# Fetching some tiles row by row from SyncE and ScalarE in two edge sums of a graph network

## The reference

```
def _rel_graph_conv(h, basis, coeff, bias, src, dst, etype, norm):
    W = jnp.einsum('rb,bdf->rdf', coeff, basis)
    Hr = jnp.einsum('nd,rdf->nrf', h, W)
    msg = Hr[src, etype] * norm
    agg = jax.ops.segment_sum(msg, dst, num_segments=N)
    return agg + bias
h = jax.nn.relu(_rel_graph_conv(feat, ...1, src, dst, etype, norm))
out = _rel_graph_conv(h, ...2, src, dst, etype, norm)
...
h = jnp.matmul(x, weight)
weighted = h[src] * edge_weight[:, None]
aggregated = jax.ops.segment_sum(weighted, tgt, num_segments=num_nodes)
in_deg = jax.ops.segment_sum(edge_weight, tgt, num_segments=num_nodes)
```

## Time and profile before

| | us |
|---|---|
| median of 3 runs | 9475.49 |
| lowest and highest | 9473.54, 9476.48 |
| the profiled execution | 9459.24 |
| its span | 9457.5 |

### The profile page before, as it was taken

The page is one execution under the profiler, slowest core; times in us unless marked ns, Lnnn a source line. Parts: engine busy times, 40 slices in busy tenths (PEclk is TensorE's granted clock), DMA queues, the critical chain, the costliest instruction groups (busy, mean ns, idle before and its releaser), DMA issues. The chain is left out here.

```text
span 9457.5 us, 158810 instructions
## 1 busy us (share of the span) xinstructions
PE 7101.5 (75%) x35186; PEld 5063.2 (54%) x35186; DVE 5926.1 (63%) x21108; ACT 3121.1 (33%) x10505; POOL 6656.1 (70%) x7024
## 2 busy tenths in 40 slices
PE   6555546666686666669999957777677777799999
PEld 4222224343343333334444446666566666799999
DVE  7666645444434444446665567777677777799888
ACT  2222210000020000000000045555455555699998
POOL 3777777777725777767777767777577777477776
PEclk9999999999995555555555567777777777899999
DMA  4222223111153111111111122222122222211111
GB/s 111 89 88 87 85 78 99 53 53 53 53 217 105 53 53 53 53 54 52 53 53 53 50 60 60 60 60 60 51 60 60 60 60 60 84 53 53 52 52 51
DMA packets 292477, 636.18 MB, mean 67 GB/s; under 512 B 124830, under 2 KB 160801, under 8 KB 279585
## 3 DMA queue, kind: packets, MB, share of 16 engines
q0 software_dynamic: 223872, 420.21, 16.8%
q1 hardware_dynamic: 68032, 210.12, 6.5%
HBM read 478.99 MB, written 150.87 MB: 67 GB/s over the span
## 5 line engine op out<-in xcount | busy, mean ns | idle before, releaser
L1058 POOL DMA_INDIRECT relsum_rows<-relation_table,tab_idx x1994 | 1891.0, 948 | 836.8 <-issue 496.1
L1101 PE MATMUL relsum_sums<-relsum_hot,relsum_rows 128*128 128x128 f32 x3988 | 1556.5, 498 | 930.8 <-DMA relsum_rows<-relation_table,tab_idx 689.0
L1101 PEld LDWEIGHTS relsum_sums<-relsum_hot,relsum_rows 128*128 128x128 f32 x3988 | 994.4, 312 | 1490.0 <-DMA relsum_rows<-relation_table,tab_idx 1477.6
L1001 POOL DMA_INDIRECT conv_rows<-tensor_table,src_idx x997 | 943.6, 946 | 404.2 <-issue 213.6
L1058 POOL DMA_INDIRECT gcnsum_rows<-x_table,src_idx x997 | 952.5, 955 | 333.5 <-issue 178.2
L1001 POOL DMA_INDIRECT gat2sum_rows<-gat_table,src_idx x997 | 944.4, 947 | 303.8 <-issue 235.5
L1001 POOL DMA_INDIRECT gat1sum_rows<-gat_table,src_idx x997 | 943.7, 947 | 303.8 <-issue 222.7
L668 POOL DMA_INDIRECT records<-sort_recs,place_rows x968 | 927.1, 958 | 295.1 <-issue 295.1
L1068 DVE TENSOR_SCALAR relsum_hot<-iota_row,dst_rel,w 128x128 f32<-128x128 f32 x1994 | 708.9, 356 | 429.1 <-issue 419.7
L1101 PE MATMUL gcnsum_sums<-gcnsum_hot,gcnsum_rows 128*128 128x128 f32 x1994 | 781.6, 495 | 0.0
L2095 ACT ACTIVATE conv_rows_attr<-conv_rows,conv_rec 128x64 f32<-128x64 f32 x2991 | 754.9, 334 | 50.5 <-SPq L2054 43.7
(11 more groups left out here) (392 smaller groups left out, 15104.0 us busy)
## 6 DMA issues: line engine op xcount, KB each, us to landing
relation_table<-table_row SPq DMA_DIRECT2D x30, 2048.0 KB, 6.3
relation_table<-sort_space SPq DMA_DIRECT2D x40, 1024.0 KB
relsum_rows<-relation_table,tab_idx POOLq DMA_INDIRECT x1994, 2.5
place_lo_wide<-lo_rows SPq DMA_DIRECT2D x121, 256.0 KB, 3.4
relation_table<-place_extra SPq DMA_DIRECT2D x20, 1024.0 KB
gcnsum_rows<-x_table,src_idx POOLq DMA_INDIRECT x997, 2.5
gat1sum_rows<-gat_table,src_idx POOLq DMA_INDIRECT x997, 2.5
gat2sum_rows<-gat_table,src_idx POOLq DMA_INDIRECT x997, 2.5
```

Of the source, the lines that this page charges most:

```text
L1001: pool.indirect_dma_start(bufs[:, t % depth, :], None, table, bass.IndirectOffsetOnAxis(ap=idx[:, t:t + 1], axis=0)).then_inc(landed[t % l ...
L1058: pool.indirect_dma_start(rows[:, t % depth, :], None, table, bass.IndirectOffsetOnAxis(ap=idx[:, t:t + 1], axis=0)).then_inc(landed[t % d ...
L1101: pe.matmul(bank[:, 0:P], rows[:, t % depth, :], hot[:, t % HOTS, :], start=True, stop=True).then_inc(s["multiplied"], 1)
```

## The change

A new class, `RowByRow`, fetches every 80th tile of a sum from another engine. It first writes the row numbers of its tiles, a few columns of the index tile, to device memory, and reads them back into one partition. For each of its tiles it then loads 16 numbers at a time into registers (8 loads) and issues 128 DMAs, each for one row of 512 bytes. It has two buffers; the fetch of its third tile and each later one waits until its tile two before is multiplied.

In the second relational sum SP fetches 12 tiles (79, 159, ... 959) and ACT 10 (119, 199, ... 839); in the graph sum SP fetches 12 (79, ... 959). POOL leaves these tiles out, its other tiles keep their buffers, and PE waits for these tiles on the semaphores of the fetching engine. The first relational sum is as it was.

```diff
+class RowByRow:
+    STEP = 80
...
+    def landed_at(self, t):
+        n = self.tiles.index(t)
+        return self.landed[n % 2], 16 * P * (n // 2 + 1)
...
+    def program(self, eng, multiplied, multiplied_at):
+        last = self.tiles[-1]
+        eng.dma_start(self.listed.rearrange("n p -> p n"), self.idx[:, self.first:last + 1:self.STEP],
+                      allow_slow_non_contiguous=True).then_inc(self.list_out, 16)
+        eng.wait_ge(self.list_out, 16)
+        eng.dma_start(self.numbers[:, :], self.listed.rearrange("(o n) p -> o (n p)", o=1)).then_inc(self.list_in, 16)
+        eng.wait_ge(self.list_in, 16)
+
+        def fetch(n, j):
+            for c in range(0, P, 16):
+                numbers = self.env.nc.values_load_multi_w_load_instructions(
+                    self.numbers[0:1, bass.ds(n * P + c, 16)], engines=[ENGINES[self.kind]], min_val=0,
+                    max_val=self.table.shape[0] - 1, skip_runtime_bounds_check_because="the records hold row numbers of the table")[1]
+                for e in range(16):
+                    eng.dma_start(self.rows[c + e:c + e + 1, j, :], self.table[bass.ds(numbers[e], 1), :]).then_inc(self.landed[j], 16)
+
+        for j in range(2):
+            fetch(j, j)
+        with eng.Fori(1, self.count // 2) as i:
+            for j in range(2):
+                eng.wait_ge(multiplied, i * (2 * self.STEP) + multiplied_at(self.first + (j - 2) * self.STEP + 1))
+                fetch(i * 2 + j, j)
...
             beside.sync(sp)
+            if "SP" in by_row:
+                by_row["SP"].program(sp, s["multiplied"], v["multiplied"])
...
                 beside.pool_at(pool, t)
+                if t in side_of:
+                    continue
...
             beside.act(act)
+            if "ACT" in by_row:
+                by_row["ACT"].program(act, s["multiplied"], v["multiplied"])
...
-                pe.wait_ge(landed[t % depth].sem, landed[t % depth].at(16 * (t // depth + 1)))
+                if t in side_of:
+                    pe.wait_ge(*side_of[t].landed_at(t))
+                    tile_rows = side_of[t].buffer(t)
+                else:
+                    pe.wait_ge(landed[t % depth].sem, landed[t % depth].at(16 * gathered(t)))
+                    tile_rows = rows[:, t % depth, :]
...
-    sum_over_slots(env, "relsum2", env.tab_idx, table, env.w1, acc[:, 0:1, :], beside=FromX())
+    sum_over_slots(env, "relsum2", env.tab_idx, table, env.w1, acc[:, 0:1, :], beside=FromX(),
+                   aside=(("SP", 79, 12), ("ACT", 119, 10)))
...
-    sum_over_slots(env, "gcnsum", env.src_idx, x_in, env.w, acc, degree=True, beside=GraphSum(env, flags, acc))
+    sum_over_slots(env, "gcnsum", env.src_idx, x_in, env.w, acc, degree=True, beside=GraphSum(env, flags, acc),
+                   aside=(("SP", 79, 12),))
```

More of the change, by code:

```diff
@@ L23 @@
 DVE_ENGINE = mybir.EngineType.DVE
+ENGINES = {"SP": mybir.EngineType.SP, "ACT": mybir.EngineType.Activation}
 P = 128
@@ L1021, in one_hots_on_act, with __init__, buffer @@
     act.activation(hot, dist[:, 0:count, :], ACT.Relu, scale=-1.0, bias=1.0).then_inc(ready, count)
-def sum_over_slots(env, tag, idx, table, weight, acc, degree=False, beside=None, banks=BANKS):
+class RowByRow:
+    STEP = 80
+    def __init__(self, env, tag, kind, first, count, idx, table, sb):
+        self.env, self.kind, self.first, self.count, self.idx, self.table = env, kind, first, count, idx, table
+        self.tiles = range(first, first + count * self.STEP, self.STEP)
+        assert count % 2 == 0 and count >= 2 and self.tiles[-1] < USED
+        self.rows = sb(f"rows_{kind}", [P, 2, D], F32)
+        self.numbers = sb(f"numbers_{kind}", [1, count * P], I32)
+        self.listed = env.nc.dram_tensor(f"{tag}_listed_{kind}", (count, P), I32, kind="Internal").ap()
+        self.list_out, self.list_in = (env.sig(f"{tag}_{n}_{kind}").sem for n in ("list_out", "list_in"))
+        self.landed = [env.sig(f"{tag}_side_landed_{kind}{j}").sem for j in range(2)]
+    def landed_at(self, t):
+        n = self.tiles.index(t)
+        return self.landed[n % 2], 16 * P * (n // 2 + 1)
+    def buffer(self, t):
+        return self.rows[:, self.tiles.index(t) % 2, :]
+    def program(self, eng, multiplied, multiplied_at):
[18 more added lines that the diff above has]
+                fetch(i * 2 + j, j)
@@ L1027, in sum_over_slots @@
+def sum_over_slots(env, tag, idx, table, weight, acc, degree=False, beside=None, banks=BANKS, aside=()):
     nc = env.nc
@@ L1041, in sum_over_slots, with gathered @@
         beside.memory(sb, ps)
+        by_row = {kind: RowByRow(env, tag, kind, first, count, idx, table, sb) for kind, first, count in aside}
+        side_of = {t: r for r in by_row.values() for t in r.tiles}
         groups = range(-(-USED // SLOT_BUFS))
+        def gathered(t):
+            return len([u for u in range(t % depth, t + 1, depth) if u not in side_of])
         block = ctx.enter_context(nc.Block(no_gpsimd_drain=True))
@@ L1100, in _ @@
                     pe.matmul(bank[0:1, P:2 * P], env.ones[:, 0:1], hot[:, t % HOTS, :], start=True, stop=True)
-                pe.matmul(bank[:, 0:P], rows[:, t % depth, :], hot[:, t % HOTS, :], start=True,
+                pe.matmul(bank[:, 0:P], tile_rows, hot[:, t % HOTS, :], start=True,
                           stop=True).then_inc(s["multiplied"], 1)
@@ L1106, in sum_over_slots @@
         for k in range(depth):
-            landed[k].passed(16 * len(range(k, USED, depth)))
+            landed[k].passed(16 * len([t for t in range(k, USED, depth) if t not in side_of]))
 def unit_blocks(u):
```

## The result

The kernel with the change takes 9443.16 us (median of 7 runs, 9438.32 to 9448.81) against 9475.49 (7 runs, 9473.35 to 9476.98): the ratio is 0.9967, 95% interval 0.9955 to 0.9978, that is 32.3 us less. The forecast was 9435, 40.2 less.

A forecast was written before the change was run, and what follows sets the result against it. POOL's gather issue was taken to bound the relational sum, PE then narrowly POOL the graph sum; -27.6 and -12.6, others 0, gave -40.2 from the 9475.5 median: 9435 us, 8-in-10 range 9428 to 9462.

The forecast's parts named there:

- Term (a): Second relational sum: 22 of 997 gathers taken off POOL, each worth 1.253 us, saving 27.6 us.
- Term (b): Graph sum: 12 gathers off POOL bring the last tile forward by 12.6 us, bounds 0 and 15.
- the fast stretch: Graph sum after the crossing matmul: at 2.4 GHz PE eats POOL's lead, in 38 us instead of 26.
- the lead of 22: Graph sum at tile 560: POOL's lead over PE grows from 15.5 to about 22.5 tiles.
- Term (c): Fetch work on SP and ACT in both sums: 90 us a fetch fits between side tiles, costing 0.
- F: Time of one side tile's fetch, 128 row DMAs and 8 register loads: 90 us, ends 67 and 134.
- The list: SP writing its row numbers in 4-byte pieces and reading them back before its first fetch: 8 us allowed.
- term (d): Transfers of the singly fetched rows: at most 0.60 of one DMA engine beside 0.19 for gathers, costing 0.
- R1: Rival: the graph sum gives nothing, PE being its bound from end to end; 9448 us, chance 15%.
- R2: Rival: fetches too slow in both sums, a chain of 12 F; 9670 or 10270 us by row cost, chance 12%.
- R3: Rival: each row DMA waits for its 2.8 us landing, +6800 us for both sums, chance 1%.
- R4: Rival: no change, as three issuing engines slow POOL's gathers by 0.03 us each, 28 us a sum; chance 3%.

The follow-up runs named there:

- the first group: Follow-up runs timed beside the unchanged kernel at 9453.11 us; the changed kernel, run again there, took 9421.09 us, ratio 0.9966.
- the third group: Follow-up runs where every sum was slower, unchanged kernel 11214.73 us; wide matmuls only 0.9996, with graph-sum fetches 1.0061, fetches in all three sums 1.1262 (wide) and 1.1280.
- the first two groups: Follow-up runs without the later general slowdown, compared with the unchanged kernel at 9453.11 us (18 runs) and 9452.22 us (13 runs).

## Why the prediction was right, and where it was off

- *Term (a), -27.6.* Right. 25.0 in the profiled pair, where a gather took 1.256 us in the one and 1.253 in the other; 26.7 in the trace and 28.0 in the time when it stood alone, where a gather took 1.250 and 1.249. One reading under it was off without harm: PE needs 0.41 us, not 0.80, for a tile whose rows are there.
- *Term (b), -12.6.* This is the term that was mis-sized: 5.8 in the profiled pair, 5.0 in the first group, 7.1 as a median of the graph part alone. It has two halves, 7 tiles more eaten in the fast stretch (8.7 us) and 386 tiles at 1.24 instead of 1.25 (3.9). The second half came, as about 5 (PE's 1.240 against 1.252 a tile behind the stretch). The first asked for a stretch of 38 us, and I took its length to be what PE needs; the row of before that I measured it by is of a stretch in which PE ran out of rows, so it couldn't show how long the clock would have stayed up. It was 30.7 us in five of the traces, 34.1 in two (the kernel before's among them), 23.9 and 44.4 in two others, and 51.2 with wide matmuls in it. With 44 us or more some 12 us came. The 38 us were also too few: they take the lead to have gone from 15.5 to nothing in 26 us, but PE's waits began with POOL still 3 to 5 tiles ahead, whose rows had not landed. With 44.4 us PE never waited, and with wide matmuls in between it first did after 48.8. Why the clock stayed up longer in one execution than in another is open.
- *What was right in it:* 560 tiles in 707.84 us, the lead of 22 at tile 560, the rise behind the crossing matmul.
- *Term (c), F = 90 us, cost nothing.* The cost was nothing, the number was too high. A row cost 0.41 us, not 0.48, and a register load 1.14, not 3.6, the figure of another engine. From one fetch to the next it was 63.8 us; of the 26 us by which that is shorter, 9 are the rows (128 x 0.07) and 17 the loads, each of which took 1.45 us with the time around it. That the time of such a sum is the number of fetches times F, once F is above the spacing, was right: with 22 fetches it came 23 us above an expectation made with an F that was 0.9 us lower, which makes 20.
- *The list.* 8 us were allowed, SP's first register load came 20 us after the list was issued, and PE's first tile was late by 14 us, which no step had: term (d) counted the rows' transfers and not the list's, beside which the DMA engines were busy for 0.99 of 16 us. Neither reached the end.
- *Term (d), 0.* Right for the rows: gathers 1.250 us apart beside three issuing engines, and the whole sum's DMA share at 0.21. A row was not spread either, of which the term had left both cases open: from 3300 to 3350 us SP's 102 rows are 204 packets, 102 of 512 bytes and 102 of 4. By the Trainium skill, "DMA: Bandwidth & Descriptors", section "Issuing engines are not separate DMA queues", spreading DMAs over engines saves only the time that the issuing sequencer takes, "usually small relative to the DMA itself". The trace agrees on what is saved, and not on its size: here the issuing engine was the bound, and the saved 1.25 us of POOL was the whole gain.
- *The rivals.* R1 (the graph sum gives nothing) is out by the traces: 5 us of pace are there, and 12 with a longer stretch. It was nearer than it looks, since 5 of 12.6 is close to the middle, and the times of the graph part alone don't exclude it. R2 didn't hold for the change as it was timed, and holds where F exceeds the spacing, by crowding (+275) or by slower issue (+66, +1423). R3 is out by the 0.408 us from row to row (its price, with its own figures, is +6880 and not +6800), R4 by the gathers.
- *Luck.* The total came nearer than its parts: 9435 was put on a median that lay 16 us above the profiled execution, without a stage that accounts for them, and the graph sum's share depends on a stretch whose length the forecast had no row for.

## What to carry to other kernels

Where one engine's issue sets the pace and others are idle, each instruction moved off it is worth its whole period, up to the rate at which the other engine can do the same work; count that rate with the issuing engine's own register loads, not with those of another. Keep such side streams well under their limit: in the third group here a fetch of 128 small DMAs grew to about twice its length while a gather grew by a seventh, and one late tile holds up all the others behind it. Check first that the engine that is relieved is still the one that the others wait for. And a stretch that ended because its work ran out doesn't tell how long it could have lasted.

## What the runs showed of the hardware that I had not expected

- Stores of 1280 and 1536 words in 4-byte pieces took 14.7 to 16.8 us to land. Beside two of them the DMA engines were busy for 0.99 of 16 us (0.17 without), and PE's first matmul came 16.4 us after the first gather, 2.5 without. It was 16.4 to 18.7 in every trace of the first two groups with such lists in the relational sum, and 2.5 to 2.6 in every one without. By the Trainium skill, "DMA: Bandwidth & Descriptors", section "Rules for kernel authors", such an access pattern lowers to one descriptor per element. The trace agrees: 1552 and 1296 packets for 1536 and 1280 words.
- In the graph sum PE with 128-column matmuls, 0.31 us from one to the next on average, busy for all of 248 us, stayed at 1.2 GHz. Behind one matmul of 512 columns it went to 2.4 GHz (a second one starts 7 to 9 us after it, inside the stretch), and fell back after 23.9 to 44.4 us with the same work going on. The length differs between executions of near-identical programs. That this is why the graph part's runs spread over 16 us is likely and not shown, since only one of them has a trace.
- Matmuls of 128 columns brought the rise as well, in the relational sum of the changed kernel, where PE had a backlog after its late start. In the trace below it made 17 of them, 0.21 us from one to the next, and then the clock was at 1.00 for 6.8 us; the other four traces of the first two groups with such a start have the same 6.8 us. So the width of 512 isn't needed for it.

```profile
2908.70:2912.40 3.70, 3.65 (x17) 3.65 (x18) 2.71 (x12) 0.00 (x0) 2.79 (x4) 0.51 0.50 148
2912.40:2919.20 6.80, 4.14 (x23) 2.89 (x22) 4.92 (x21) 0.00 (x0) 5.27 (x6) 1.00 0.23 62
```

- The mean granted clock of the changed kernel was 0.726 in one run and 0.789 in another, at 9443.06 and 9443.03 us: where the clock differed, it did not set the time. Which stages those are isn't known, for only the first has a trace.
